# A reworked front for a stencil and mixture-of-experts kernel, with its experts' operands at multiples of 2 KB in SBUF

## The chip, the cores and the metric

One core of a Trainium2 chip runs one program. The metric is device time in microseconds, the median of the runs. Compared are the kernel before and the same kernel with the change below.

## What is computed

The reference takes `x` of shape (8, 128, 128), a step length per batch, and an index per batch. First it makes one explicit step of an advection-diffusion equation on every 128 x 128 grid, and cuts it off at zero:

```
Af = A_grid[None] * f[:, None];  Bf = B_grid[None] * f[:, None]
gradv_Af  = _grad(Af[:, 0], 1) + _grad(Af[:, 1], 2)
gradvv_Bf = _grad2(Bf[:, 0], 1) + _grad2(Bf[:, 1], 2) + _grad(_grad(Bf[:, 2], 2), 1) + _grad(_grad(Bf[:, 2], 1), 2)
x = maximum(f + (-gradv_Af + gradvv_Bf * 0.5) * dt[:, None, None], 0.0)
```

Then each grid is read as 128 tokens of 128 features. `h` is `x` normalised over the features, normalised again over the tokens, and scaled and shifted by `gamma` and `beta`, which a small four-layer network makes from the batch's index. A router picks two of eight experts for each token, and each expert has a hidden layer of 512:

```
gates, idx = top_k(softmax(h @ router_w), 2);  gates = gates / gates.sum(-1)
hid = relu(einsum('nd,edf->nef', h, exp_w1) + exp_b1)
eout = einsum('nef,efd->ned', hid, exp_w2) + exp_b2
out = x + einsum('ned,ne->nd', eout, combine)
```

## The kernel before

Everything is one tile of 128 partitions. The 8 batches are two halves of 4; the 1,024 tokens lie along the free axis. Each engine runs a list of instructions in the order written in its block (`block.sync` for the loads, `block.gpsimd`, `block.scalar`, `block.tensor`, `block.vector`), and semaphores join the lists; nothing is reordered by a planner.

**The front.** Differences along rows and columns are matmuls with two constant matrices, `diff` and `neg_half_diff2`. Each half needs five products of `f` or its transpose `ft` with a grid (`s_b2`, `u_a0`, `u_b0`, `u_a1`, `u_b1`): VectorE makes them for half 0, GpSimd three of them for half 1. `step_cross` makes the inner difference of the mixed term, `cross_operand` its operand `wT`, and `rows_a`, `rows_b`, `columns_b`, `columns_w` add the step up in PSUM (`yt` for half 0, `aux` for half 1). `advance` (L788) multiplies that by the step length and takes `f` away, `relu_step` (L411) cuts it off into `xs`. `feature_stats`, `inverse_sd_features` and `normalise` make `xn`, `norm_transposed` (L586) transposes it, and `token_stats`, `inverse_sd_tokens`, `scale_and_shift` and `conditioned` make `h`. `refined` (L803) is one Newton step for the reciprocal root that ScalarE found by logarithm and exponential. Four small matmuls (`net_layer`, L530) and one pair at L708 and L709 make the style; ScalarE's steps between them are `embedded`, `hyper_first`, `hyper_second`, `style_first` and `softplus`. `step_transposed` and `transposed_step` put the transposed step into `acc`, for the final sum. `keep_warm` (L525) issues matmuls whose result nobody reads.

**The experts.** Expert 0 works in plain fp32, by halves: `layer1_0` (L614) and `layer2_0` (L619), with the second half's front between the first half's matmuls. Experts 1 to 7 work in fp32r with split operands: `h_hi` + `h_lo`, `ws` (weights, high and low part, two slots) and `hid_hi` + `hid_lo`, three matmuls for each product (L625 to L627, and L649, L650, L653). ScalarE makes `hid_hi` and `hid`, VectorE `hid_lo`; hidden layers run three chunks ahead of the output layers. The last expert's output layer is cut into parts of 512, 256 and 256 tokens, `y_last` (L200), so that the stores can start early.

**SBUF.** `sb` (L82) declares a buffer; each takes its bytes in a partition, rounded up to 32, and lies right behind the one declared before it. The operands in question are `h`, `h_hi`, `h_lo` (L133 to L135), and `ws`, `hid`, `hid_hi`, `hid_lo` (L170 to L173).

## Time and profile before

| | us |
|---|---|
| median of 3 runs | 119.5 |
| lowest and highest | 119.18, 119.82 |
| span of the profiled execution | 117.9 |

In the page's part on busy shares an engine's entry is its busy time, the share of the span, and the number of instructions. The line on PEclk cuts the span into 40 equal slices and gives TensorE's granted clock in tenths of full speed; a 9 is 90% or more. In the chain of waits a row is a start, a length and the work that ended last there, in order of time. In a timeline a row is a start, a length and an instruction, or several merged (`x4`); what stands in brackets is the engine's idle time before it and who ended it. An fp32 matmul stands as two records.

### The profile page before, as it was taken

Reading aid. Unit: us, or ns where it says so; the run is one execution under the profiler, and the core shown is the slowest. Engines: PE = TensorE matmul, PEld = TensorE weight load, DVE = VectorE, ACT = ScalarE, POOL = GpSimd, SP = SyncE. Lnnn points to the kernel's source line nnn. Section 1 sums busy time; section 2 is a strip of 40 time slices with the busy share of each in tenths; the row PEclk is TensorE's granted clock in tenths of the full one; section 3 lists DMA queues with packets and bytes.
Section 4 is the critical chain, followed back from the end, with each engine's and each line's share of the span. In section 5 each row is a group of like instructions: output and inputs, shape, how many; then the busy total and the mean of one; then the engine's idle time right before and its main releaser. Section 6 shows DMA issues by size and latency. Waiting matters only on the chain.

```text
span 117.9 us, 1519 instructions
## 1 busy us (share of the span) xinstructions
PE 111.9 (95%) x506; PEld 85.0 (72%) x506; DVE 91.8 (78%) x198; ACT 75.5 (64%) x99; POOL 8.8 (7%) x18
## 2 busy tenths in 40 slices
PE   6999999998999999999999999999999999999960
PEld 2469894446646688888888888888888888888850
DVE  0398789748993496999959976996799589879781
ACT  0403456756361997777777777777777777777800
POOL 1437430000000000000000000000000000000040
PEclk9999999999999999999999999999999999999998
DMA  2999991000000270050400040021004000500004
GB/s 94 310 366 418 407 407 47 0 0 0 0 0 6 96 266 0 8 178 0 178 0 0 29 152 0 0 120 64 0 0 178 0 0 8 170 0 6 0 0 178
DMA packets 4583, 10.86 MB, mean 92 GB/s; under 512 B 800, under 2 KB 1888, under 8 KB 4576
## 3 DMA queue, kind: packets, MB, share of 16 engines
q1 hardware_dynamic: 3920, 9.93, 22.4%
q10 hardware_dynamic: 656, 0.84, 2.3%
q8 instruction: 4, 0.07, 0.2%
q14 instruction: 3, 0.02, 0.1%
HBM read 10.21 MB, written 0.56 MB: 91 GB/s over the span
## 4 chain that ended last, share of the span: by engine, by line
PE 84%; DVE 7%; DMA 4%; issue 1%; ACT 1%; SPq 0%; DVEq 0%
PE zt L625 11%; PE zt L626 11%; PE zt L627 11%; PE zt L614 6%; PE aux L653 6%; PE aux L650 6%; PE aux L649 6%; PE yt L653 5%; PE yt L650 5%; PE yt L649 5%; PE yt L619 4%; DMA gn<-in_grids_dram 4%; DVE st L824 2%; DVE h L853 1%; PE aux L574 1%; PE zt L543 1%
## 5 line engine op out<-in xcount | busy, mean ns | idle before, releaser
L498 ACT ACTIVATE hid_hi<-zt,pv 128x1024 fp32r<-128x1024 f32 x27 | 30.2, 1120 | 17.4 <-PE zt L627 17.3
L945 DVE TENSOR_TENSOR hid_lo<-hid,hid_hi 128x1024 fp32r<-128x1024 f32 x27 | 33.0, 1221 | 10.0 <-issue 5.4
L503 ACT ACTIVATE hid<-zt,pv 128x1024 f32<-128x1024 f32 x27 | 29.9, 1108 | 0.0
L625 PE MATMUL zt<-h_hi,ws 128*128 128x512 f32 x56 | 22.7, 406 | 0.0
L626 PE MATMUL zt<-h_hi,ws 128*128 128x512 f32 x56 | 21.8, 390 | 0.0
L627 PE MATMUL zt<-h_lo,ws 128*128 128x512 f32 x56 | 21.8, 389 | 0.0
L625 PEld LDWEIGHTS zt<-h_hi,ws 128*128 128x128 f32 x56 | 10.5, 188 | 3.0 <-issue 0.5
L626 PEld LDWEIGHTS zt<-h_hi,ws 128*128 128x128 f32 x56 | 10.5, 188 | 2.5 <-issue 0.5
L627 PEld LDWEIGHTS zt<-h_lo,ws 128*128 128x128 f32 x56 | 10.5, 188 | 2.2
L650 PE MATMUL aux<-hid_hi,ws 128*128 128x512 f32 (+1 forms) x32 | 12.0, 376 | 0.0
L649 PE MATMUL aux<-hid_hi,ws 128*128 128x512 f32 (+1 forms) x32 | 12.0, 376 | 0.0
L653 PE MATMUL aux<-hid_lo,ws 128*128 128x512 f32 (+1 forms) x32 | 12.0, 376 | 0.0
L649 PE MATMUL yt<-hid_hi,ws 128*128 128x512 f32 (+1 forms) x28 | 10.5, 374 | 0.0
L650 PE MATMUL yt<-hid_hi,ws 128*128 128x512 f32 (+1 forms) x28 | 10.5, 374 | 0.0
L653 PE MATMUL yt<-hid_lo,ws 128*128 128x512 f32 (+1 forms) x28 | 10.5, 374 | 0.0
L968 DVE TENSOR_TENSOR acc<-acc,yg 128x512 f32<-128x512 f32 x14 | 9.0, 685 | 0.0
L875 DVE TENSOR_TENSOR ws<-we,ws 128x1024 fp32r<-128x1024 f32 x7 | 8.6, 1225 | 0.2
L370 POOL TENSOR_TENSOR acc<-acc,yg 128x512 f32<-128x512 f32 x1 | 1.3, 1272 | 96.3 <-DVE yg L1003 96.3
L614 PE MATMUL zt<-h,we 128*128 128x512 f32 x16 | 7.6, 607 | 0.6 <-DVE h L853 0.6
L619 PE MATMUL yt<-hid,we 128*128 128x512 f32 x16 | 7.5, 592 | 0.0
L528 PE MATMUL zt<-warm 128*128 128x512 bf16 x18 | 6.0, 485 | 1.2 <-DVE warm L775 1.2
L873 DVE CAST ws<-we 128x1024 fp32r<-128x1024 f32 x7 | 4.8, 691 | 2.8 <-PE yt L653 1.4
(136 smaller groups left out, 143.0 us busy)
## 6 DMA issues: line engine op xcount, KB each, us to landing
we<-in_exp_w_dram SPq DMA_DIRECT2D x8, 512.0 KB, 9.1
gate_all<-gates_dram SPq DMA_DIRECT2D x8, 512.0 KB, 3.5
f<-in_x_dram SPq DMA_DIRECT2D x2, 256.0 KB, 4.5
ft<-in_x_exchanged_dram ACTq DMA_DIRECT2D x2, 256.0 KB, 5.3
out_dram<-acc SPq DMA_DIRECT2D x1, 256.0 KB, 2.1
out_dram<-acc SPq DMA_DIRECT2D x2, 128.0 KB, 2.0
first<-d_difference_dt_ids_dram ACTq DMA_DIRECT2D x1, 136.0 KB, 3.2
gn<-in_grids_dram SPq DMA_DIRECT2D x1, 128.0 KB, 4.4
```

The source lines that it names most:

```text
L498: act.activation(hid_hi[:, c, :], zt[c % 2][:], ACT.Relu, bias=bias).then_inc(hi_ready, 1)
L503: act.activation(hid[:, c, :], zt[c % 2][:], ACT.Relu, bias=bias).then_inc(hid_ready, 1)
L614: pe.matmul(z0[c], we[:, 0, 0, c, :], h[:, half(n)], start=True, stop=True).then_inc(z0_ready, 1)
L619: pe.matmul(yt[:, half(n)], we[:, 0, 1, c, :], hid[:, c, half(n)], start=(c == 0), stop=(c == C - 1)).then_inc(l2_0_done, 1)
L625: pe.matmul(zt[c % 2][:, tok], w_hi, h_hi[:, tok], start=True, stop=False)
L626: pe.matmul(zt[c % 2][:, tok], w_lo, h_hi[:, tok], start=False, stop=False)
L627: return pe.matmul(zt[c % 2][:, tok], w_hi, h_lo[:, tok], start=False, stop=True)
L649: pe.matmul(out_ps, w_hi, hid_hi[:, c, tok], start=(c == 0), stop=False)
L650: pe.matmul(out_ps, w_lo, hid_hi[:, c, tok], start=False, stop=False)
L653: return pe.matmul(out_ps, w_hi, hid_lo[:, c, tok], start=False, stop=(c == C - 1))
L945: v.tensor_tensor(hid_lo[:, c, :], hid[:, c, :], hid_hi[:, c, :].bitcast(F32), ALU.subtract).then_inc(lo_ready, 1)
L968: v.tensor_tensor(acc[:, half(n)], acc[:, half(n)], yg[:, half(n)], ALU.add).then_inc(acc_half, 1)
```

## The change

Of the front:

- The loads are dealt out anew between the queues of SP and ACT. `ln_g` and `ln_b` come with the first load, and GpSimd makes four values from them.
- The second half's step is made whole in PSUM. ScalarE scales `diff` and `neg_half_diff2` by minus each batch's step length, an identity matmul puts in `f`, and ScalarE takes the ReLU from PSUM. `advance` remains for half 0 only.
- The Newton steps are folded: the last factor is applied to products made beside the earlier steps. `gamma` is one VectorE operation, no longer four on GpSimd.
- TensorE's order: the transposes of half 0's `xn` come before the style network's last layer and most of half 1's step; those of half 1's `xn` after one `layer2_0`, not two. The first hidden matmul is cut into two pairs of batches. Both `keep_warm` calls behind the first are gone.
- ScalarE's order: see the diff. `cross_product` makes `s_b2` of half 0 in two parts.

Of the layout: two unused buffers, `ahead_of_h` (800 bytes in a partition) and `ahead_of_ws` (1,632 bytes).

The diff, cut to its core:

```diff
-        neg_xp = sb("neg_xp", [P, B, P])
+        diff_dt = sb("diff_dt", [P, BH, P])
+        neg_half_diff2_dt = sb("neg_half_diff2_dt", [P, BH, P])
+        neg_dt = sb("neg_dt", [P, B])
+        neg_xp = sb("neg_xp", [P, BH, P])
...
+        ahead_of_h = sb("ahead_of_h", [P, 200])
         h = sb("h", [P, T])
         h_hi = sb("h_hi", [P, T], F32R)
         h_lo = sb("h_lo", [P, T], F32R)
...
+        ahead_of_ws = sb("ahead_of_ws", [P, 408])
         ws = sb("ws", [P, SLOTS, 2, 2, C, P], F32R)
         hid = sb("hid", [P, C, T])
         hid_hi = sb("hid_hi", [P, C, T], F32R)
...
             load(f[:, 0:BH, :], x[:, 0:BH, :], f_in[0])
             load(gn[:], grids, gn_in)
-            load(gt[:], gridsT, gt_in)
-            load(neg_half_diff2, second_diff, diff2_in)
+            load(ft[:, 0:BH, :], xT[:, 0:BH, :], ft_in[0])
             load(f[:, BH:B, :], x[:, BH:B, :], f_in[1])
+            load(ft[:, BH:B, :], xT[:, BH:B, :], ft_in[1])
+            load(pw[:], p64, p64_in)
+            load(ident, identity, ident_in)
             load(pv[:], p128, p128_in)
...
+            pool.tensor_scalar(gsq[:], ln_g, ln_g, 0.25, ALU.mult, ALU.mult).then_inc(gain_ready, 1)
+            pool.tensor_scalar(quarter_g[:], ln_g, 0.25, None, ALU.mult).then_inc(gain_ready, 1)
+            pool.tensor_scalar(minus_quarter_g[:], ln_g, -0.25, None, ALU.mult).then_inc(gain_ready, 1)
+            pool.tensor_scalar(half_b[:], ln_b, 0.5, None, ALU.mult).then_inc(gain_ready, 1)
...
-            product(u_b0, f, gn[:, 1, :]).then_inc(b0_ready[1], 1)
             pool.wait_ge(ft_in[1], 16)
             pool.wait_ge(gt_in, 16)
             product(u_a1, ft, gt[:, 1, :]).then_inc(a1_ready[1], 1)
+            product(u_b0, f, gn[:, 1, :]).then_inc(b0_ready[1], 1)
+            pool.wait_ge(a0_ready[1], 1)
             product(u_b1, ft, gt[:, 0, :]).then_inc(b1_ready[1], 1)
 
-            pool.wait_ge(glog_ready, 1)
-            step(pool.tensor_tensor(gsum[:], gpos[:], glog[:], ALU.add))
-            step(pool.tensor_scalar(gamma[:], gsum[:], 1e-8, None, ALU.add))
-            pool.wait_ge(p128_in, 16)
-            pool.tensor_scalar(half_gamma[:], gamma[:], 0.5, None, ALU.mult).then_inc(gamma_ready, 1)
-            pool.tensor_scalar(gamma_g[:], gamma[:], ln_g, 0.25, ALU.mult, ALU.mult).then_inc(gamma_ready, 1)
...
-            act.dma_start(ft[:, 0:BH, :], xT[:, 0:BH, :]).then_inc(ft_in[0], 16)
-            act.dma_start(pw[:], p64).then_inc(p64_in, 16)
-            act.dma_start(ft[:, BH:B, :], xT[:, BH:B, :]).then_inc(ft_in[1], 16)
-            act.dma_start(ident, identity).then_inc(ident_in, 16)
+            act.dma_start(gt[:], gridsT).then_inc(gt_in, 16)
+            act.dma_start(neg_half_diff2, second_diff).then_inc(diff2_in, 16)
             act.preload_act_table_set("natural_log_exp_and_others")
+
+            def scaled_differences():
+
+                act.wait_ge(first_in, 16)
+                act.activation(neg_dt[:], dtb, ACT.Copy, scale=-1.0).then_inc(neg_dt_ready, 1)
+                act.wait_ge(neg_dt_ready, 1)
+                for b in range(BH, B):
+                    act.activation(diff_dt[:, b - BH, :], diff, ACT.Copy, scale=neg_dt[:, b:b + 1]).then_inc(diff_dt_ready, 1)
+                act.wait_ge(diff2_in, 16)
+                for b in range(BH, B):
+                    act.activation(neg_half_diff2_dt[:, b - BH, :], neg_half_diff2, ACT.Copy,
+                                   scale=neg_dt[:, b:b + 1]).then_inc(diff2_dt_ready, 1)
...
+            def relu_whole_step(k):
+
+                act.wait_ge(df_ready, BH // 2 + k + 1)
+                b = BH + 2 * k
+                act.activation(xs[:, b:b + 2, :].rearrange("p b j -> p (b j)"), pair_of(1, k),
+                               ACT.Relu).then_inc(xs_ready, 1)
...
             act.wait_ge(const_ready, 2)
+            scaled_differences()
+            relu_step(0)
             embedded()
-            relu_step(0)
             relu_step(2)
             hyper_first()
+            inverse_sd_features(0)
             hyper_second()
-            inverse_sd_features(0)
+            normalise(0)
             style_first()
-            normalise(0)
             softplus()
             inverse_sd_tokens(0)
             transposed_step(0)
             conditioned(0)
-            relu_step(4)
-            relu_step(6)
+            relu_whole_step(0)
+            relu_whole_step(1)
             hidden0(0, 0)
...
             inverse_sd_tokens(1)
+            conditioned(1)
             transposed_step(1)
-            conditioned(1)
...
+            def whole_step_input(k):
+
+                pe.wait_ge(ident_in, 16)
+                pe.wait_ge(f_in[1], 16)
...
+                pe.matmul(pair_of(1, k), ident, f[:, b:b + 2, :].rearrange("p b j -> p (b j)"),
+                          start=True, stop=False, skip_group_check=True)
+
+            def whole_step_rows_b():
+
+                pe.wait_ge(b0_ready[1], 1)
+                pe.wait_ge(diff2_dt_ready, BH)
+                for b in range(BH, B):
+                    pe.matmul(own(b), neg_half_diff2_dt[:, b - BH, :], u_b0[:, b, :], start=False, stop=False,
+                              skip_group_check=True)
...
+                pe.wait_ge(a0_ready[1], 1)
+                for b in range(BH, B):
+                    pe.matmul(own(b), diff_dt[:, b - BH, :], u_a0[:, b, :], start=False, stop=False,
+                              skip_group_check=True)
...
+            def whole_step_columns_w():
+
+                pe.wait_ge(w_op_ready, 2)
+                pe.wait_ge(diff_dt_ready, BH)
+                for b in range(BH, B):
+                    pe.matmul(own(b), wT[:, b, :], diff_dt[:, b - BH, :], start=False, stop=False, skip_group_check=True)
...
+            def whole_step_columns_b(k):
+
+                pe.wait_ge(b1_ready[1], 1)
+                for b in of_pair(1, k):
+                    last = pe.matmul(own(b), u_b1[:, b, :], neg_half_diff2_dt[:, b - BH, :], start=False, stop=True,
+                                     skip_group_check=True)
+                last.then_inc(df_ready, 1)
...
+            def layer1_0_by_pairs():
+
+                for k, made in enumerate((h_ready, h_act_ready)):
+                    pe.wait_ge(made, 2)
+                    tok = slice(2 * k * P, 2 * (k + 1) * P)
+                    last = pe.matmul(z0[0][:, tok], we[:, 0, 0, 0, :], h[:, tok], start=True, stop=True)
+                last.then_inc(z0_ready, 1)
...
-            rows_b(1, 0, start=True)
+            whole_step_input(0)
             pe.wait_ge(p128_in, 16)
             net_layer(2, pv[:, HW2_AT:HW2_AT + SH], hyp1[:], SH)
-            rows_b(1, 1, start=True)
+            whole_step_input(1)
             net_layer(3, pv[:, SW1_AT:SW1_AT + SE], hyp2[:], SE)
-            columns_w(1, 0, final=False)
+            whole_step_rows_b()
+            pe.wait_ge(xp_ready, BH)
+            norm_transposed(0)
             pe.wait_ge(net_sb, 4)
             pe.matmul(small[:, 0:B], pw[:, SW2_AT:SW2_AT + P], sty1[:], start=True, stop=True)
             pe.matmul(small[:, B:2 * B], pw[:, SW2_AT + P:SW2_AT + 2 * P], sty1[:], start=True,
                       stop=True).then_inc(net_ps, 1)
-            columns_w(1, 1, final=False)
-            pe.wait_ge(ident_in, 16)
-            pe.wait_ge(xp_ready, BH)
-            norm_transposed(0)
-            columns_b(1)
+            whole_step_columns_w()
+            whole_step_rows_a()
             step_transposed(0)
-            rows_a(1, start=False)
-
-            keep_warm(WARM_H[0])
-            wait_for_h(0)
+            whole_step_columns_b(0)
+            whole_step_columns_b(1)
+
             pe.wait_ge(net_sb, 6)
+            pe.wait_ge(w_in[0], 16)
+            layer1_0_by_pairs()
             pe.wait_ge(acc_ready, 1)
-            pe.wait_ge(w_in[0], 16)
-            for c in range(C):
+            for c in range(1, C):
                 layer1_0(0, c)
             layer2_0(0, 0)
-            layer2_0(0, 1)
-            pe.wait_ge(xp_ready, B)
+            pe.wait_ge(xs_ready, BH)
             norm_transposed(1)
-            layer2_0(0, 2)
-            layer2_0(0, 3)
+            for c in range(1, C):
+                layer2_0(0, c)
             step_transposed(1)
             logits(0)
-            keep_warm(WARM_H[1])
             wait_for_h(1)
...
-            def refined(n, variance, eps, rough, sq, vs, rs):
+            def normalise(n):
 
                 hb = batches(n)
-                then(v.tensor_tensor(sq[:, hb], rough[:, hb], rough[:, hb], ALU.mult))
-                then(v.scalar_tensor_tensor(vs[:, hb], variance, eps, sq[:, hb], ALU.add, ALU.mult))
-                then(v.scalar_tensor_tensor(rs[:, hb], vs[:, hb], 3.0, rough[:, hb], ALU.subtract, ALU.mult))
-
-            def normalise(n):
-
                 v.wait_ge(var1_ready, BH * (n + 1))
                 v.wait_ge(rs1_ready, n + 1)
-                refined(n, mv1[:, batches(n), 1], 1e-5, rough1, sq1, vs1, rs1)
-                v.scalar_tensor_tensor(mrs1[:, batches(n)], mv1[:, batches(n), 0], -1.0, rs1[:, batches(n)], ALU.mult,
+                squared = mark(v.tensor_tensor(sq1[:, hb], rough1[:, hb], rough1[:, hb], ALU.mult))
+                mark(v.scalar_tensor_tensor(rm1[:, hb], mv1[:, hb, 0], -1.0, rough1[:, hb], ALU.mult, ALU.mult))
+                v.wait_ge(dve, squared)
+                then(v.scalar_tensor_tensor(vs1[:, hb], mv1[:, hb, 1], 1e-5, sq1[:, hb], ALU.add, ALU.mult))
+                v.scalar_tensor_tensor(rs1[:, hb], vs1[:, hb], 3.0, rough1[:, hb], ALU.subtract,
+                                       ALU.mult).then_inc(rs1_final, 1)
+                v.scalar_tensor_tensor(mrs1[:, hb], vs1[:, hb], 3.0, rm1[:, hb], ALU.subtract,
                                        ALU.mult).then_inc(mrs1_ready, 1)
+                v.wait_ge(rs1_final, n + 1)
                 for b in range(n * BH, n * BH + XN_DVE):
                     v.tensor_scalar(xn[:, b, :], xs[:, b, :], mv1[:, b, 0:1], rs1[:, b:b + 1], ALU.subtract,
...
                 v.tensor_scalar(ve2[:, batches(n)], mv2[:, batches(n), 1], gsq[:, 0:1], 1e-8, ALU.mult,
                                 ALU.add).then_inc(var2_ready, 1)
-                then(v.tensor_scalar(mh[:, batches(n)], mv2[:, batches(n), 0], minus_half_g[:, 0:1], ln_b, ALU.mult,
-                                     ALU.add))
-                v.wait_ge(gamma_ready, 2)
-                return mark(v.scalar_tensor_tensor(tg[:, batches(n)], mh[:, batches(n)], ln_b, half_gamma[:, batches(n)],
-                                                   ALU.subtract, ALU.mult))
+                last = mark(v.tensor_scalar(mh[:, batches(n)], mv2[:, batches(n), 0], minus_quarter_g[:, 0:1],
+                                            half_b[:, 0:1], ALU.mult, ALU.add))
+                if n == 0:
+                    v.wait_ge(glog_ready, 1)
+                    v.wait_ge(net_sb, 5)
+                    last = mark(v.scalar_tensor_tensor(gamma[:], gpos[:], 1e-8, glog[:], ALU.add, ALU.add))
+                v.wait_ge(dve, last)
+                return mark(v.scalar_tensor_tensor(tg[:, batches(n)], mh[:, batches(n)], half_b[:, 0:1],
+                                                   gamma[:, batches(n)], ALU.subtract, ALU.mult))
...
-                refined(n, ve2[:, hb], 0.0, rough2, sq2, vs2, rs2)
+                squared = mark(v.tensor_tensor(sq2[:, hb], rough2[:, hb], rough2[:, hb], ALU.mult))
+                mark(v.scalar_tensor_tensor(rg2[:, hb], rough2[:, hb], quarter_g[:, 0:1], gamma[:, hb], ALU.mult,
+                                            ALU.mult))
                 v.wait_ge(dve, moved)
-                shifted = mark(v.tensor_tensor(shift0[:, hb], tg[:, hb], rs2[:, hb], ALU.mult))
-                v.tensor_tensor(scale[:, hb], rs2[:, hb], gamma_g[:, hb], ALU.mult).then_inc(shift_ready, 1)
+                mark(v.tensor_tensor(rt2[:, hb], rough2[:, hb], tg[:, hb], ALU.mult))
+                v.wait_ge(dve, squared)
+                then(v.tensor_tensor(vs2[:, hb], ve2[:, hb], sq2[:, hb], ALU.mult))
+                shifted = mark(v.scalar_tensor_tensor(shift0[:, hb], vs2[:, hb], 3.0, rt2[:, hb], ALU.subtract, ALU.mult))
+                v.scalar_tensor_tensor(scale[:, hb], vs2[:, hb], 3.0, rg2[:, hb], ALU.subtract,
+                                       ALU.mult).then_inc(shift_ready, 1)
                 v.wait_ge(dve, shifted)
                 v.wait_ge(net_sb, 6)
                 v.tensor_tensor(shift[:, hb], shift0[:, hb], beta[:, hb], ALU.add).then_inc(shift_ready, 1)
...
+            cross_product(0)
+            cross_product(1)
...
-            advance(0)
-            v.wait_ge(p128_in, 16)
-            mark(v.tensor_scalar(gsq[:], ln_g, ln_g, 0.25, ALU.mult, ALU.mult))
-            squared = mark(v.tensor_scalar(minus_half_g[:], ln_g, -0.5, None, ALU.mult))
+            advance()
...
             product(u_a0, f, 1, gn[:, 0, :]).then_inc(a0_ready[1], 1)
-            v.wait_ge(dve, squared)
             moved = token_stats(0)
             scale_and_shift(0, moved)
             conditioned(0)
-            advance(1)
             feature_stats(1)
```

## Rows read from the trace of the kernel before

**Rows 1.** The page: busy time of the engines, and granted clock by slice.
```profile
PE 111.9 (95%) x506; PEld 85.0 (72%) x506; DVE 91.8 (78%) x198; ACT 75.5 (64%) x99; POOL 8.8 (7%) x18
...
PEclk9999999999999999999999999999999999999998
```

**Rows 2.** TensorE in two stretches: length, busy, instructions, clock, DMA share, GB/s.
```profile
29.18:113.90 84.72, 84.69 (x372) 1.00 0.14 51
5.50:19.60 14.10, 13.67 (x89) 1.00 0.91 351
```

**Rows 3.** The chain of waits, in the front.
```profile
1.16 4.36 DMA gn<-in_grids_dram
...
8.54 0.89 PE yt L568 x8
...
18.66 0.74 DVE h L853 x2
19.57 3.67 PE zt L614 x8
...
29.18 1.10 PE zt L614 x2
```

**Rows 4.** Timeline of TensorE in the front.
```profile
7.41 1.13 PE L561 MATMUL yt<-u_b,neg_half_diff 128*128 128x256 f32 x4
...
13.15 0.28 PE L533 MATMUL zt<-hyp,pv 128*64 128x8 f32 x2
...
15.09 0.60 PE L594 MATMUL yt<-ident,xn 128*128 128x128 f32 x4
...
17.72 1.67 PE L528 MATMUL zt<-warm 128*128 128x512 bf16 x7
...
24.80 0.60 PE L594 MATMUL aux<-ident,xn 128*128 128x128 f32 x4
...
28.20 0.59 PE L528 MATMUL zt<-warm 128*128 128x512 bf16 x2
```

**Rows 5.** The DMA view: KB, and us from issue to landing.
```profile
gn<-in_grids_dram SPq DMA_DIRECT2D x1, 128.0 KB, 4.4
```

**Rows 6.** Timeline of VectorE in the front.
```profile
10.96 0.20 DVE L915 TENSOR_SCALAR gsq<-pv 128x1 f32<-128x1 f32 x1
...
11.14 0.87 DVE L798 BATCH_NORM_STATS2 st<-xs 128x6 f32<-128x128 f32 x4
12.05 0.38 DVE L801 BATCH_NORM_AGGREGATE mv<-st 128x2 f32<-128x6 f32 x4
...
17.68 0.16 DVE L806 TENSOR_TENSOR sq<-rough 128x4 f32<-128x4 f32 x1
...
19.31 1.12 DVE L792 SCALAR_TENSOR_TENSOR neg_xp<-aux,first,f 128x128 f32<-128x128 f32 x4
```

**Rows 7.** Timeline of ScalarE in the front.
```profile
12.89 0.28 ACT L419 ACTIVATE lv<-mv,eps_ln 128x4 f32<-128x4 f32 x1
...
17.55 0.58 ACT L447 ACTIVATE acc<-zt 128x512 f32<-128x512 f32 x1
```

**Rows 8.** Timeline of TensorE in the block and in the last expert.
```profile
42.80 0.39 PE L625 MATMUL zt<-h_hi,ws 128*128 128x512 f32 x1
...
44.16 0.39 PE L649 MATMUL aux<-hid_hi,ws 128*128 128x512 f32 x1
...
110.89 0.40 PE L649 MATMUL aux<-hid_hi,ws 128*128 128x512 f32 x1
111.13 0.40 PE L650 MATMUL aux<-hid_hi,ws 128*128 128x512 f32 x1
...
112.64 0.28 PE L649 MATMUL aux<-hid_hi,ws 128*128 128x256 f32 x1
...
113.00 0.28 PE L649 MATMUL yt<-hid_hi,ws 128*128 128x256 f32 x1
...
113.36 0.28 PE L649 MATMUL yt<-hid_hi,ws 128*128 128x256 f32 x1
```

## What the change was predicted to do

> **What bounds the kernel now.** I read the page's busy shares first: TensorE (PE) is busy for 95% of the span, at a granted clock of nine tenths or more in nearly every slice [rows 1]. The chain of waits then says from when. It follows one load and a string of short links through VectorE (DVE), ScalarE (ACT) and PE until 29.18 us, where the second half's `h` reaches PE [rows 3]; behind that point PE is busy for 84.69 of 84.72 us, to the last matmul [rows 2]. So the kernel is a front of 29.18 us, a closed block of PE work of 84.7 us, and an end of 4.0 us (117.9 - 113.9). The time falls by what the start of the block moves forward, and by what changes inside the block. The profiled execution spans 117.9 us, the median run is 119.5 us; I keep the 1.6 us between them.
>
> **The block.** Nothing in it is reordered. What changes is where its operands lie. In the kernel before, a buffer starts at the next multiple of 32 bytes behind the one declared before it; this puts `h`, `h_hi` and `h_lo` 1,056 bytes past a multiple of 2,048, and `ws`, `hid`, `hid_hi` and `hid_lo` 1,568 bytes past one. With the declarations that are added and dropped and the two pads of 800 and 1,632 bytes, all of them come to 0. So every 512-column operand (2,048 bytes) crosses a 2,048-byte line before, and none does after. Six block matmuls stand between the starts 42.80 and 44.16, which is 226.7 ns each [rows 8]. The last expert tests whether the crossing is what costs: it has operands of 256 columns, those of the `aux` part run from 1,568 across the line to 2,592, those of the `yt` part from 544 to 1,568, inside it. Three `aux` ones take from 112.64 to 113.00, and three `yt` ones from there to 113.36 [rows 8]: 0.12 us each, on either side. The distances between moving operand and weights don't change modulo 512 bytes either. I cost the edit at 0 for 324 matmuls of 512 columns and 24 of 256. Its bounds are not closed by this: only an absolute start of 32 modulo 64 bytes has been seen for these operands, and none of 0. Below, a bf16 matmul of the same 512 columns comes every 0.216 us (seven in 1.67, two in 0.59) [rows 4], 10.7 ns less, which makes 348 x 10.7 = -3.7 us; above, two block matmuls once stand 0.24 apart (110.89 to 111.13) [rows 8], and 348 x 8 to 13 ns would be +2.9 to +4.6 us. I take 0, since the row that varies the crossing shows no effect.
>
> The Trainium skill ("TensorE: Matmul & The Clock Gate", section "Back-to-back issue gap") gives N/2.4 + 2.5 ns for a matmul at full clock, 215.8 ns for 512 columns. By it the block's 226.7 ns is not the engine's own pace, and something, of which the start address is one candidate, would be giving 10.9 ns back; the bf16 rows agree with the page, the block's rows do not.
>
> **The front, first half, up to the transposes of `xn`.** (a) The loads are dealt out anew. `gn` lands 4.4 us after its issue, at 5.5 us [rows 3, 5], with the 256 KB of `ft` behind `first` on ACT's queue; now only the 128 KB of `gt` ride there, and `neg_half_diff2` is issued third on ACT instead of fourth on SP. `rows_b` had started at 7.41, when it had landed [rows 4]. `gn` may gain nothing or 0.4 us, the stall behind `neg_half_diff2` another 0.15; I take -0.5, bounds -0.1 and -0.7. The eight scaled matrices are 8 ACT operations of about 0.4 us plus one small one, 3.5 us on an ACT queue that holds nothing else until 10.6; if `neg_half_diff2` were late they end by 9, still in that cover. (b) `gsq` and `minus_half_g` leave DVE for GpSimd (POOL): 11.14 - 10.96 = -0.18 [rows 6]; POOL has 2.5 us to spare there. (c) `inverse_sd_features(0)` stood behind `hyper_second`: its first operation ran at 12.89 [rows 7], the variances were there at 12.43 (12.05 + 0.38) [rows 6]. Now it is ahead: -0.45. Together -1.1 on the DVE and ACT side. PE had to give as well, since the transposes at 15.09 came straight behind `columns_w(1, 1)` [rows 4]: between network layer 3 (13.15) [rows 4] and 15.09 it did two groups of 4 matmul records, four small ones and their bubbles, now one group of 8, which costs 0.89 [rows 3] and 0.1 to refill. I take -1.15 for the transposes, at 13.95.
>
> **First half, from there to the hidden layer.** (d) `refined` was three dependent steps of 0.2 us and two more (17.68 to 18.66) [rows 3, 6]; its last step is folded into `scale` and `shift0`: -0.15. POOL's four operations for gamma go, for one DVE step of 0.2 us beside `mh`; in turn the style network's last layer is behind the transposes, so the logarithm ends some 0.1 before it is used. Nothing on balance, at worst +0.3. (e) A new cost: `step_transposed(0)` is now behind `whole_step_columns_w` and `whole_step_rows_a`, 0.89 us each. ACT's copy of its result, 0.58 us, ran in the gap at 17.55 while DVE made the scales [rows 7]. Now it gets its input at about 17.1 and stands in ACT's queue ahead of the two `h` of `conditioned(0)`, which are due at 17.2: +0.35, bounds 0 and +0.6. DVE's two `h` aren't behind it, and `layer1_0_by_pairs` lets PE begin with them, but PE's next 0.43 us need ACT's pair. So the second pair starts at 19.57 - 1.15 - 0.15 + 0.35 = 18.62. `keep_warm(7)` only filled the wait (17.72 to 19.4) [rows 4]: removed at no gain.
>
> **Second half.** (f) The step is now whole inside PSUM, so DVE's four `neg_xp`, 1.12 us [rows 6], go and the two ReLUs follow ACT's `h` directly: the features side comes 1.4 us earlier and has `xn` by 22.75 (24.15 before). (g) The transposes of `xn` move ahead of one more `layer2_0` (0.86 us): they start at 18.62 + 0.43 + 2.58 + 0.86 + 0.1 = 22.6, held to 22.75, against 24.80. From them to `layer1_0(1, 0)` it took 29.18 - 24.80 = 4.38; less 0.15 as in (d), `h` is ready at 27.0. (h) But PE itself: from the start of these transposes to the second `keep_warm` it went from 24.80 to 28.20 [rows 4], 3.4 us of dense work; now one `layer2_0` of 0.86 more lies there: 22.75 + 3.4 + 0.86 = 27.0, and 0.1 for a bubble. The two meet; what is late next is PE itself, and the second `keep_warm` (0.43, at 28.20) has no room to be missed. The block starts at 27.1 instead of 29.18: **-2.1 us**. With (a) and (e) at their bounds it is -0.9 to -2.8. Inside the block `h_hi`, `h_lo` and the first split weights follow `h` at the old distance, and their matmuls wait for them 2 us less than they have to spare.
>
> The sum: 117.9 - 2.1 + 0 = 115.8 us of span, and with 1.6 us around it 117.4 us. By its own bounds, 116.7 to 118.6.
>
> **The rivals.** *The block speeds up*: if the start address is what holds the matmuls at 226.7 ns, they fall to 216: 117.4 - 3.7 = 113.7 us. For it speaks the bf16 row; against it the last expert's two kinds of start. *The block slows down*, the one that ends on the other side: with all operands at the same 2,048-byte phase, the moving read, the weight load behind it and the writes of DVE and ACT may meet in the same place. It decides from 2.1 us / 348 = 6 ns a matmul on; at 0.235 us each, which PE shows only when it starts anew [rows 8], it is +2.9: 120.3 us. Against it: `hid`, its parts and `ws` shared one phase before as well. *The front gains little*: the ACT queue takes the place of DVE. The copy of (e) and `hidden0(0, 0)` (0.67 us) stand ahead of the two small operations on which the second half's `xn` hangs, and `gn` may land no earlier; then the block starts at 28.3 to 29.2, and the time is 118.6 to 119.5 us. *The clock falls*: PE now has nine warming matmuls less and waits of 0.3 us between small network layers. The clock stayed full over the 14.1 us of this stretch with 13.67 busy [rows 2]; with PE at the lower of its two levels for the first group of the hidden layer, its 3.67 us [rows 3] double, some +2.9 us after what the other engines hide: 120.3 us. The Trainium skill (same page, section "HAM oscillation — how this bites in real kernels") warns of gaps between bursts, which speaks against taking these matmuls out; no row here shows a fall.
>
> **How the numbers follow.** The forecast of 117.4 has 0.62, a front that gains little 0.18, a faster block 0.10, a slower block 0.06, the clock 0.04. The range 116.2 to 119.5 leaves out the last three, 0.20 together. A measurement of this kernel can tell about 0.5% (0.6 us) from no change: faster is 0.62 + 0.10 + a third of 0.18 = 0.78, same 0.12, slower 0.10.
>
> **What would show it.** In the profile after: the last DVE-waiting `layer1_0` start at 27.1; the `h` rows of DVE near 17.2 and 26; no `neg_xp` of the second half; the copy of `zt` to `acc` just before ACT's first `h`; six block matmuls in 1.36 us. If they take 1.30 or 1.41, the block's part is wrong; if the start is beyond 28.3, so is the front's, most likely at (e) or (a).

## The result, and the profile after

The changed kernel took 117.48 us (117.08 to 118.07, 4 runs) beside 119.34 us for the kernel before (119.16 to 119.82, 4 runs): a ratio of 0.984, with a 95% interval of 0.980 to 0.987. The forecast was 117.4. The profiled execution took 117.48 us and spans 115.7 us; before it was 117.9 us. The ratios here and below leave out executions more than 1.5% longer than the fastest of their kernel, two in all: one of 120.78 us with the late transposes and one of 121.65 us with the new loads.

The page of the kernel after, its first part and the granted clock, beside [rows 1]:

```profile
PE 110.6 (96%) x511; PEld 85.7 (74%) x511; DVE 90.5 (78%) x198; ACT 78.0 (67%) x108; POOL 9.5 (8%) x18
...
PEclk9999999999999999999999999999999999999997
```

The chain of waits of the kernel after, in part, from its beginning to the start of the block, beside [rows 3] (start, length, what ended last):

```profile
1.17 3.93 PE zt L559 x9
...
5.13 1.13 PE zt L574 x8
...
17.50 0.89 PE aux L640 x8
...
26.46 0.79 PE yt L671 x8
27.26 0.97 PE zt L679 x2
```

The chain of before ran over a load, VectorE and ScalarE; this one is TensorE alone from 5.13 us on. No other engine stands in it any more. Small waits remain inside its groups, which the chain doesn't name (0.23 us at the first `h`, below). The timeline of TensorE in the front has the milestones that the prediction named, beside [rows 4] (start, length, instruction):

```profile
5.13 1.13 PE L574 MATMUL zt<-first,s_b 128*128 128x128 f32 x8
6.10 1.03 PE L582 MATMUL yt<-u_a,first 128*128 128x256 f32 x4
...
13.87 0.67 PE L660 MATMUL yt<-ident,xn 128*128 128x128 f32 x4
...
18.24 1.34 PE L686 MATMUL zt<-h,we 128*128 128x256 f32 x4
...
22.85 0.60 PE L660 MATMUL aux<-ident,xn 128*128 128x128 f32 x4
...
27.12 1.10 PE L679 MATMUL zt<-h,we 128*128 128x512 f32 x2
```

So the block starts at 27.12 us instead of 29.18 [rows 2], 2.06 us sooner, and the rest of the span is as long as it was: the second half's first `layer1_0` to the last matmul, in the view by stretches (stretch, length, busy, clock, DMA share, GB/s), beside the first row of [rows 2]:

```profile
27.12:111.81 84.69, 84.67 (x374) 1.00 0.14 51
```

### The profile page after: what moved, and what is told of

Read it like the earlier page. It is cut to its first block, busy times and chain, and to the rows that moved or that the text cites. A ratio compares the mean times of both kernels' runs of the same rounds, so it can differ in the third digit from the quotient of the medians.

```text
span 115.7 us, 1540 instructions
## 1 busy us (share of the span) xinstructions
PE 110.6 (96%) x511; PEld 85.7 (74%) x511; DVE 90.5 (78%) x198; ACT 78.0 (67%) x108; POOL 9.5 (8%) x18
## 3 DMA queue, kind: packets, MB, share of 16 engines
HBM read 10.21 MB, written 0.56 MB: 93 GB/s over the span
## 4 chain that ended last, share of the span: by engine, by line
PE 96%; DVE 1%; DVEq 0%; issue 0%
PE zt L698 11%; PE zt L699 11%; PE zt L700 11%; PE yt L692 6%; PE aux L723 6%; PE aux L722 6%; PE aux L726 6%; PE zt L679 5%; PE yt L723 5%; PE yt L722 5%; PE yt L726 5%; PE zt L559 3%; PE zt L574 2%; PE yt L671 1%; PE zt L686 1%; PE aux L619 1%
## 5 line engine op out<-in xcount | busy, mean ns | idle before, releaser
L722 PEld LDWEIGHTS aux<-hid_hi,ws 128*128 128x128 f32 x32 | 6.0, 188 | 1.2
L723 PEld LDWEIGHTS aux<-hid_hi,ws 128*128 128x128 f32 x32 | 6.0, 188 | 1.2
```

What stands on the lines that cost most here:

```text
L722: pe.matmul(out_ps, w_hi, hid_hi[:, c, tok], start=(c == 0), stop=False)
L723: pe.matmul(out_ps, w_lo, hid_hi[:, c, tok], start=False, stop=False)
```

## The experiments

Two questions. Does the layout edit do anything, since the block neither gained nor lost? And do the steps of the front work as they were costed? All runs keep the whole computation. In the table below a buffer's place is its start in a partition modulo 2,048 bytes, and a block stretch always holds the same 288 matmuls, from the start of the 23rd split-weight matmul to that of the 311th: 287 of 512 columns and one of 256. The kernel before took 119.6 to 119.7 us in the sessions of these runs, beside 119.34 when the changed kernel was measured. So kernels of different sessions are compared by their ratios.

### The layout

**The changed front without the pads.**

```
-        ahead_of_h = sb("ahead_of_h", [P, 200])
-        ahead_of_ws = sb("ahead_of_ws", [P, 408])
```

> The changed kernel without its two pads: h and its parts start 1,248 bytes, ws and the hid buffers 1,664 bytes past a multiple of 2,048. Theory (the start address costs nothing): six block matmuls in 1.36 us as before and after, block start near 27.1 us, median 117.5 us. Rival (the pads repair a slower block that the new declarations made): six take 1.40 us or more, and the time is 119 us or more.

119.81 us, ratio 1.002 (0.999 to 1.004). The whole gain is gone, though the block starts at 27.44 us. Its matmuls come more slowly, so the rival held.

**The changed front with the operands where they stood before** (`h` and its parts at 1,056, `ws` and `hid` at 1,568): the pads are `[P, 464]` and `[P, 24]`.

> The changed kernel with pads that put h at 1,056 and ws and the hid buffers at 1,568 bytes past a multiple of 2,048, as in the kernel before: the front's edits alone. Theory: 117.5 us, six block matmuls in 1.36 us. Rival (a part of the gain is the layout's): between 118 and 119.3 us.

118.01 us, ratio 0.985 (0.981 to 0.990): the gain is there without any multiple of 2 KB. The time lies at the edge of the rival's range, but the layout isn't what puts it there: the block stretch is the same (below). In the profiled execution the block starts 0.51 us later than in the kernel after, and TensorE's first group alone takes 0.53 us more (6.62 - 5.12 = 1.50 us, against 0.97).

**The kernel before with its operands at multiples of 2 KB**, by pads of 248 and 384 elements at the same two places.

> The kernel before with two pads (992 and 1,536 bytes) that put all the experts' operands at multiples of 2,048 bytes: the layout's edit alone. Theory: 119.4 us, no change, 1.36 us for six. Rival: 118.8 us or less.

119.68 us, ratio 0.999 (0.997 to 1.002). For the kernel before, this layout is worth nothing.

**One distance only: `ws` at 288**, everything else at 0.

```
-        ahead_of_ws = sb("ahead_of_ws", [P, 408])
+        ahead_of_ws = sb("ahead_of_ws", [P, 480])
+        ahead_of_hid = sb("ahead_of_hid", [P, 440])
```

> The changed kernel with ws 288 bytes past a multiple of 2,048 and everything else at one, so that weights and moving operands no longer stand at the same place modulo 512 bytes, and the weights are at 32 modulo 64. Theory (neither absolute nor relative places matter): 117.5 us, 1.36 us for six. Rival (the relative place matters, and was the same in both kernels): another spacing, 1.30 us (113.8 us in all) if 226.7 ns was already the slow one, 1.40 us or more (119 us or more) if it was the fast one.

119.75 us, ratio 1.001 (0.998 to 1.004): the relative place matters, and 226.7 ns was the faster pace.

**All at 1,664**, the place that `ws` and `hid` had without pads: `ahead_of_h` is `[P, 104]`, and `ahead_of_ws` stays at 408.

> The changed kernel with h, h_hi, h_lo, ws, hid, hid_hi and hid_lo all 1664 bytes past a multiple of 2,048 (1664 is where ws and hid stood in the kernel without pads, e1_after_no_pads; there h stood at 1248). Theory A, what counts is that the weights and the moving operand of a block matmul stand at one and the same place modulo 512 bytes, wherever that is: every spacing in the block falls back to 226.7 ns (544 periods of 2.4 GHz) and the time to 117.5 us (117.2 to 118.1), ratio 0.984 to 0.990. Theory B, what counts is where ws itself stands (fast at 0 and 32 modulo 512, as in the runs so far, slow at 128 and 288): the spacing stays at 231 to 233 ns, as in the hid groups of e1_after_no_pads, where ws and hid stood equal and the mean was 231.4 ns, and the time at 119.2 to 119.9 us, ratio about 1.000. Theory C, that only multiples of 2 KB are sure: as B. I hold A at 55 in 100.

117.56 us, ratio 0.984 (0.978 to 0.989), as by theory A.

**`ws` at 64**, everything else at 0: pads `[P, 200]`, `[P, 424]`, and `ahead_of_hid` with 496 elements.

> The changed kernel with ws alone moved to 64 bytes past a multiple of 2,048; h, h_hi, h_lo, hid, hid_hi and hid_lo at 0. The fast kernels so far had weights and moving operands at equal places modulo 512 bytes, and the slow ones had them 288 (e4_after_ws_288) and 96 (the h groups of e1_after_no_pads) bytes apart: both are 32 more than a multiple of 64. Theory A1, the two need only agree modulo 64 bytes: spacing 226.7 ns and 117.5 us (117.2 to 118.1), ratio 0.984 to 0.990. Theory A2, they must agree more coarsely than that (modulo 128, 256 or 512): spacing 233.3 ns (560 periods of 2.4 GHz) and 119.7 us (119.2 to 119.9), ratio 0.997 to 1.004. I hold A1 at 50 in 100.

120.18 us, ratio 1.003 (1.001 to 1.005), as by theory A2.

The same 288 block matmuls in these kernels, one row of the view by stretches each. In this order: the kernel after, the old places, all at 1,664 (the fast ones); without pads, `ws` at 288, `ws` at 64 (the slow ones):

```profile
40.26:105.43 65.17, 65.17 (x289) 1.00 0.16 58
```

```profile
40.80:105.97 65.17, 65.17 (x289) 1.00 0.16 57
```

```profile
40.22:105.38 65.16, 65.16 (x289) 1.00 0.17 59
```

```profile
40.62:107.54 66.92, 66.92 (x289) 1.00 0.16 58
```

```profile
40.55:107.63 67.08, 67.08 (x289) 1.00 0.15 57
```

```profile
40.81:107.90 67.09, 67.09 (x290) 1.00 0.15 56
```

TensorE is busy throughout at a clock of 1.00 in all six, and still 1.75 to 1.92 us go. The profile names no wait for it; each matmul comes a little later behind the last. Six of them in the kernel with `ws` at 64, and six in the kernel after:

```profile
44.08 0.40 PE L699 MATMUL zt<-h_hi,ws 128*128 128x512 f32 x1
...
45.48 0.40 PE L723 MATMUL aux<-hid_hi,ws 128*128 128x512 f32 x1
```

```profile
43.44 0.39 PE L698 MATMUL zt<-h_hi,ws 128*128 128x512 f32 x1
...
44.80 0.39 PE L722 MATMUL aux<-hid_hi,ws 128*128 128x512 f32 x1
```

45.48 - 44.08 = 1.40 us against 1.36: 233.3 ns each instead of 226.7. In one table (the mean is over the 287 gaps of 512-column matmuls in the stretch; the times are of several sessions):

| kernel | `h` parts | `ws` | `hid` parts | distance, modulo 512 | ns a matmul | median, us |
|---|---|---|---|---|---|---|
| before | 1056 | 1568 | 1568 | 0 | 226.7 | 119.34 |
| before, at 2 KB | 0 | 0 | 0 | 0 | 226.7 | 119.68 |
| after | 0 | 0 | 0 | 0 | 226.7 | 117.48 |
| after, old places | 1056 | 1568 | 1568 | 0 | 226.7 | 118.01 |
| after, all at 1,664 | 1664 | 1664 | 1664 | 0 | 226.7 | 117.56 |
| after, no pads | 1248 | 1664 | 1664 | 96 for `h` | 232.8 | 119.81 |
| after, `ws` at 288 | 0 | 288 | 0 | 288 for all | 233.3 | 119.75 |
| after, `ws` at 64 | 0 | 64 | 0 | 64 for all | 233.3 | 120.18 |

What decides is not where an operand stands but where weights and moving operand stand towards each other. The absolute place is out: 0, 1,056/1,568 and 1,664 are all fast. Crossing a line of 2,048 bytes is out too, since all 512-column operands of the kernel at 1,664 cross one. A distance of 64, 96 or 288 bytes is slow, a multiple of 512 is fast. Since all weight tiles of a slot lie 512 bytes apart and serve the same moving operand, no coarser step than 512 can matter; whether 128 or 256 would do wasn't tried.

The price falls on the matmuls of 512 columns alone. The last expert's last twelve have 256; their first and last start, in the kernel after and in the one with `ws` at 288:

```profile
110.20 0.28 PE L722 MATMUL aux<-hid_hi,ws 128*128 128x256 f32 x1
...
111.51 0.28 PE L726 MATMUL yt<-hid_lo,ws 128*128 128x256 f32 x1
```

```profile
112.43 0.28 PE L723 MATMUL aux<-hid_hi,ws 128*128 128x256 f32 x1
...
113.74 0.28 PE L727 MATMUL yt<-hid_lo,ws 128*128 128x256 f32 x1
```

Both are 1.31 us for eleven steps, 119 ns each; with `ws` at 64 it is 1.29 us (112.66 to 113.95).

Two things stay open. The first is the mechanism: the runs show the distance that costs, but not whether TensorE's two reads meet or something else does. The second: without pads `hid` and `ws` stand at the same place, yet their matmuls are slow too (a mean of 231.4 ns, those with `h` 234.2). With `h` moved to that place as well, all are at 226.7. Either a group of `h` matmuls slows the group of `hid` matmuls behind it, or the distance between `h` and `hid` counts as well; in the other two slow kernels these two stand at the same place. These runs don't separate the two.

### The front

**Both `keep_warm` calls put back** (`keep_warm(7)` ahead of `layer1_0_by_pairs`, `keep_warm(2)` behind `logits(0)`).

> The changed kernel with both groups of warming matmuls put back, seven ahead of the first hidden matmul and two behind the logits of half 0. Theory (TensorE itself is the last to be ready in the changed front, so nothing hides them): 7 x 0.216 less about 0.15 of wait, and 2 x 0.216, is +1.8 us: block start 28.9 us, 119.3 us. Rival (there is slack of other engines' making left, as in the kernel before): at most +0.6 us.

119.33 us, ratio 0.996 (0.993 to 0.999): 0.012 of 119.7 us, 1.5 us of the gain, are lost, near the 1.8 that the theory gave. The same nine matmuls taken out of the kernel before:

> The kernel before without its nine warming matmuls behind the first stage. Theory (they only fill waits): 119.4 us, block start 29.2 us, granted clock full. Rival (they keep the clock up): the lower of the two clock levels shows in the slices behind them, six block matmuls or the first hidden ones take up to twice as long, 120.3 us or more.

119.66 us, ratio 1.001 (0.998 to 1.002). So they cost nothing before and 1.5 of their 1.9 us (9 x 0.216) after. The chain of the kernel after with `keep_warm` back shows why; they are on it:

```profile
18.27 1.46 PE zt L559 x6
19.73 0.86 PE zt L686 x4
...
28.27 0.45 PE zt L559 x2
28.71 0.43 PE zt L679
```

And without them the clock doesn't fall in the kernel before. It ran at this granted clock, and the first hidden group behind a wait of 1.68 us takes 3.51 us to the next group's start (22.76 - 19.25), as with them (23.08 - 19.57):

```profile
core 0: 117.5 us, clock 1.000
```

```profile
19.25 3.67 PE L614 MATMUL zt<-h,we 128*128 128x512 f32 x8 [1.68 <-ACT h L441]
```

**The transposes of half 1's `xn` behind two `layer2_0`**, as before the change.

```
             layer2_0(0, 0)
+            layer2_0(0, 1)
             pe.wait_ge(xs_ready, BH)
             norm_transposed(1)
-            for c in range(1, C):
+            for c in range(2, C):
```

> The changed kernel with the transposes of half 1's xn after two layer2_0 again, not one. Theory (h of half 1 and TensorE meet within 0.1 us at the block's start): h comes 0.86 us later, and TensorE waits for it: +0.8 us, block start 27.9 us, 118.3 us. Rival (TensorE's amount of work alone sets the start): 0, 117.5 us.

118.28 us, ratio 0.987 (0.982 to 0.992). TensorE now reaches the block first and waits for `h`:

```profile
24.46 0.60 PE L660 MATMUL aux<-ident,xn 128*128 128x128 f32 x4
...
28.73 0.67 PE L679 MATMUL zt<-h,we 128*128 128x512 f32 x1 [0.72 <-DVE h L938]
```

From the transposes to the block it is 4.27 us, as in the kernel after (27.12 - 22.85). So in the kernel after TensorE's list and the making of `h` end together, and one more `layer2_0` ahead of the transposes goes through whole.

This profiled execution is the one of 120.78 us; the other three took 118.06 to 118.34. It lost a further 1.7 us behind the block's start, where six matmuls of `layer1_0` take 4.35 us (30.48 to 34.83) instead of 2.66 (28.87 to 31.53 in the kernel after). The granted clock was low there (stretch, length, busy, clock, DMA share, GB/s):

```profile
30.48:34.83 4.35, 4.35 (x8) 0.61 0.00 0
```

The front readings lie ahead of that stretch and aren't touched by it. Whether the wait of 0.72 us brought the fall on isn't shown: waits of 0.83 us at the same place and of 1.68 us, in the kernel before without its fillers, were followed by none.

**ScalarE's copy of the step behind its two `h`** (`conditioned(0)` ahead of `transposed_step(0)`).

> The changed kernel with ScalarE's copy to acc behind its two h of half 0, not ahead of them. Theory: the h pair is ready at 18.1 us, not 18.8, TensorE's bubbles of 0.3 us there shrink to 0.1: -0.2 us, 117.3 us. Rival (the copy is awaited by the second hidden matmul, or the ReLUs behind it are late next): 0 or up to +0.4 us.

117.99 us, ratio 0.986 (0.981 to 0.991). The 117.3 of the theory didn't come; what the edit did is read from the profile below.

**`hyper_second` and `style_first` of ScalarE back ahead of the features' work.**

```
-            inverse_sd_features(0)
             hyper_second()
-            normalise(0)
+            inverse_sd_features(0)
             style_first()
+            normalise(0)
```

> The changed kernel with ScalarE's old order of half 0: inverse_sd_features(0) behind hyper_second, normalise(0) behind style_first. Theory: the logarithm runs at 12.4 to 12.5 us, not 11.9; the transposes of xn and all behind them come 0.5 us later: 118.0 us. Rival (TensorE's rows_b group, which ends just before the transposes, covers it): 0 to +0.1 us.

118.21 us, ratio 0.986 (0.980 to 0.992).

None of these three ratios is clear of the changed kernel's own 0.984 (0.980 to 0.987), so what follows rests on one profiled execution of each. Nor can they be read from the start of the block alone, because the profiled executions differ in something else: TensorE's first group of eight took 0.97 us in the kernel after (5.13 to 6.10, above), and 1.84 us with the copy late, 1.64 us with ScalarE's order back, 1.68 us with the late transposes. The copy's kernel, timeline of TensorE:

```profile
5.00 2.05 PE L574 MATMUL zt<-first,s_b 128*128 128x128 f32 x8
6.84 1.09 PE L582 MATMUL yt<-u_a,first 128*128 128x256 f32 x4
...
14.66 0.67 PE L660 MATMUL yt<-ident,xn 128*128 128x128 f32 x4
...
19.03 1.10 PE L686 MATMUL zt<-h,we 128*128 128x256 f32 x4
19.97 2.74 PE L679 MATMUL zt<-h,we 128*128 128x512 f32 x6
...
23.40 0.60 PE L660 MATMUL aux<-ident,xn 128*128 128x128 f32 x4
```

The eight records stand 0.21 us apart here and 0.11 us in the kernel after, half the pace until 6.8 us. That is the ratio of the engine's two clock levels, and I take it for the lower one, though the row of the granted clock reads 1.00 here. It is the same code up to there. With TensorE last from 5 us on, this delay goes through to the block whole, as in the kernel with the old places, and it has to be taken off before the edit can be read. So the later intervals decide. The first hidden group takes 0.94 us (19.97 - 19.03) instead of 1.17 (19.41 - 18.24, the kernel after): the copy costs TensorE 0.23 us where it stands ahead of ScalarE's `h`. From the first `xn` transposes to that group's start it is 4.37 us in both. For ScalarE's order, the start of the first group is later by 0.33 us and the group itself longer by 0.67; behind that its milestones are 15.05, 19.64, 24.26 and 28.53:

```profile
15.05 0.90 PE L660 MATMUL yt<-ident,xn 128*128 128x128 f32 x4
...
28.53 0.67 PE L679 MATMUL zt<-h,we 128*128 128x512 f32 x1
```

28.53 - 27.12 - 0.33 - 0.67 = 0.41 us for the order. For the late transposes 28.73 - 27.12, less 0.05 and 0.71, is 0.85 us, one `layer2_0`.

**The new order of the loads in the kernel before.**

```
-            load(gt[:], gridsT, gt_in)
-            load(neg_half_diff2, second_diff, diff2_in)
-            load(f[:, BH:B, :], x[:, BH:B, :], f_in[1])
+            load(ft[:, 0:BH, :], xT[:, 0:BH, :], ft_in[0])
+            load(f[:, BH:B, :], x[:, BH:B, :], f_in[1])
+            load(ft[:, BH:B, :], xT[:, BH:B, :], ft_in[1])
+            load(pw[:], p64, p64_in)
+            load(ident, identity, ident_in)
...
-            act.dma_start(ft[:, 0:BH, :], xT[:, 0:BH, :]).then_inc(ft_in[0], 16)
-            act.dma_start(pw[:], p64).then_inc(p64_in, 16)
-            act.dma_start(ft[:, BH:B, :], xT[:, BH:B, :]).then_inc(ft_in[1], 16)
-            act.dma_start(ident, identity).then_inc(ident_in, 16)
+            act.dma_start(gt[:], gridsT).then_inc(gt_in, 16)
+            act.dma_start(neg_half_diff2, second_diff).then_inc(diff2_in, 16)
```

> The kernel before with the loads dealt out over the two queues in the changed order (ln_g and ln_b still with the 128-row parameters). Theory: gn lands 0.3 to 0.7 us earlier, the stall behind neg_half_diff2 goes, block start 28.7 us, -0.5 us: 118.9 us. Rival (something behind it, TensorE's rows in half 0 or the later products, takes the gain back): -0.1 us or less.

119.63 us, ratio 0.999 (0.995 to 1.002). Its timeline of TensorE, and its DMA view:

```profile
5.47 1.13 PE L543 MATMUL zt<-first,s_b 128*128 128x128 f32 x8 [0.37 <-DVE s_b L780]
...
7.38 1.13 PE L561 MATMUL yt<-u_b,neg_half_diff 128*128 128x256 f32 x4
...
15.06 0.60 PE L594 MATMUL yt<-ident,xn 128*128 128x128 f32 x4
```

```profile
first<-d_difference_dt_ids_dram ACTq DMA_DIRECT2D x1, 136.0 KB, 3.8
gn<-in_grids_dram SPq DMA_DIRECT2D x1, 128.0 KB, 3.6
...
neg_half_diff<-n_second_difference_dram ACTq DMA_DIRECT2D x1, 64.0 KB, 5.7
```

The rival held. `gn` lands 0.8 us sooner than in [rows 5] (3.6 us from its issue; in the kernel before without fillers, with the old loads, it is 3.7 as well, so most of this is no matter of the order). But `first` is later (3.8 us from its issue, 3.2 before), so that `step_cross` starts at 5.47, and `neg_half_diff2` is no sooner, so that `rows_b` starts at 7.38, where it was 7.41 [rows 4]. The transposes of `xn` are at 15.06 (15.09 before). In the kernel after, issued at the same time in the same order, `neg_half_diff2` needed 4.5 us. Why it took 5.7 here stays open.

## Why the prediction was right

**The total and its path: right.** 115.7 us of span against 115.8 forecast, 117.48 us against 117.4. The milestones: transposes of half 0 at 13.87 (13.95 forecast), of half 1 at 22.85 (22.75), the block at 27.12 (27.1). "What is late next is PE itself" holds, and earlier than I had it, from 5.13 us and not only from the second half: put back, the nine fillers move the block from 27.12 to 28.55 us, although TensorE's first matmuls started 0.17 us sooner in that execution. The other kernels with this front say the same. Where the first group takes 0.97 us, the block starts 21.98 or 21.99 us behind `step_cross`: 27.12 - 5.13 in the kernel after, 27.44 - 5.46 without pads, 27.38 - 5.39 with `ws` at 288, 27.07 - 5.09 at 1,664, 27.63 - 5.64 with `ws` at 64. What varies between executions is when `step_cross` starts and at what pace. That the profiled execution met the forecast to 0.1 us is therefore partly luck: with the same front the block starts anywhere from 27.07 to 27.63 us.

**(a) the loads: the size held, what makes it is more than their order.** I took -0.5 us, and -1.15 for the whole way to the transposes of `xn`. Half 0's step ends where the network's first layer begins, in the kernel before and in the one after:

```profile
10.25 0.28 PE L533 MATMUL zt<-onehot,pw 32*64 32x8 f32 x2
```

```profile
9.71 0.28 PE L564 MATMUL zt<-onehot,pw 32*64 32x8 f32 x2
```

That is -0.54 us. `step_cross` starts 0.22 us later (4.91 before, 5.13 after), but the waits for `u_a0` and `neg_half_diff2` are gone: from `step_cross` to this row it took 5.34 us and takes 4.58. From here to the transposes it is 4.16 us instead of 4.84 (15.09 in [rows 4]): another -0.68 from TensorE's own order and from ScalarE's, which has `xn` ready for it (with ScalarE's old order the transposes are 0.18 us later, 15.05 - 13.87 less the two delays). Together -1.22. The order of loads alone, in the kernel before, brought nothing: there `step_cross` was at 5.47 and `rows_b` still waited. Two things differ: in the kernel after, VectorE makes `s_b` for `step_cross` in two parts, and `neg_half_diff2` took 1.2 us less to land. So the loads' share rests on the whole change, and no run shows it alone. Its size isn't sure either: that row starts at 9.95 to 10.25 us in the three profiles with the old loads and front, and at 9.53 to 10.21 in the six with the new ones and a first group of 0.97 us. What holds in all of these six is the missing waits: 4.57 or 4.58 us from `step_cross` to this row, where the old ones take 4.69 to 5.34.

**(b), (c), (d).** `gsq` is made on GpSimd at 7.82 us, far ahead of its use. Undoing ScalarE's order (c, with `style_first`) costs 0.41 us; I had 0.45 on that side. From the transposes to VectorE's `h` it takes 3.49 us (17.36 - 13.87) instead of 3.57 (18.66 - 15.09), half of the 0.15 of (d). The folded Newton step and `gsq` weren't tried alone.

**(e) the copy: right in kind, 0.23 us instead of 0.35, and the step around it 0.26 us off.** It stands where I put it, waits for TensorE, and ends last ahead of ScalarE's pair of `h`:

```profile
17.53 0.60 ACT L477 ACTIVATE acc<-zt 128x512 f32<-128x512 f32 x1 [1.08 <-PE zt L649]
18.03 0.80 ACT L471 ACTIVATE h<-yt,shift,scale 128x128 f32<-128x128 f32 x2
```

TensorE's second pair of batches starts here:

```profile
18.88 0.70 PE L686 MATMUL zt<-h,we 128*128 128x256 f32 x2
```

The forecast had 18.62. I had let ScalarE's `h` alone set this point; VectorE's `h` was being made from 17.36 on, but TensorE's own list ran to 18.24. From the second pair to the transposes of half 1 it takes 3.97 us (22.85 - 18.88) instead of the 4.13 that I added up, and so the milestones behind it agree again to 0.1.

**The fillers: "removed at no gain" holds for the kernel before (1.001) and not for the new order (0.996 instead of 0.984).** I costed the removal against the waits of before; the cover was what the rest of the change took away.

**(f) to (h): right.** The second half's features side is early enough, and with one more `layer2_0` ahead of the transposes `h` comes 0.72 us too late for TensorE. That the clock doesn't fall was right for the four executions of this kernel (117.08 to 118.07 us). The rival is real all the same: with the late transposes one execution in four had the fall, for about 1.7 us.

**The block at 0: right, for one of two reasons.** The sentence that carries is the one I gave second: "the distances between moving operand and weights don't change modulo 512 bytes". The crossing of the 2,048-byte line agrees with the result (0.999 for the kernel before at multiples of 2 KB) but isn't what matters. The last expert's 256-column matmuls, my test for it, couldn't have shown a cost of placement: they come every 119 ns in the slow kernels too. What I missed is the comparison in between. The front's new and dropped declarations move every buffer behind them; without the pads `h` would stand 96 bytes off `ws` modulo 512, the block would lose 1.75 us in the stretch shown, and the kernel would be at 119.81. So the layout edit is worth about 2 us beside the same front without it, and nothing beside the kernel before: 0.018 in the ratios, or 2.1 us. The profiled spans differ by 2.2 us, 1.8 of them in the block and 0.3 by a first load that landed later in that execution. The rival "the block slows down" gave 0.235 us a matmul, near the 0.2328 to 0.2333 of the slow kernels, and had the condition reversed: I had feared that equal places collide, and it is unequal ones that cost. The rival "speeds up to 216 ns" falls: no layout went below 226.7.

The Trainium skill ("SBUF — State Buffer", section "Who interferes with whom") has it that TensorE has two independent read ports, one for the moving operand and one for the weights, and never waits on anyone. It says nothing on placement. Read as a rule that TensorE's reads are never held up, it would leave no layout a cost, and the trace disagrees: 6.7 ns a matmul, 65.17 against 67.09 us over 288.

## What to carry to other kernels

A new or dropped buffer is part of a change even when nobody reads it: it shifts what is declared behind it. Where TensorE streams fp32r matmuls of 512 columns back to back, with a weight load each, hold weights and moving operands a multiple of 512 bytes apart, and compare the spacing of the matmuls in the block whenever the list of buffers changes; the busy share and the clock don't show it. Cost the removal of a filler against the waits that the new order leaves, not those of the old. And before a row is used as a test, ask whether the effect would show in it at all: matmuls of 256 columns don't feel the placement.

## What was not expected of the hardware

- Relative place: 64, 96 or 288 bytes between weights and moving operand, modulo 512, cost 6.1 to 6.7 ns for each matmul of 512 columns (226.7 to 232.8 or 233.3 ns), at a granted clock of 1.00 and with TensorE 100% busy. Those of 256 columns come every 119 ns either way.
- TensorE's rise to full clock at the beginning comes at a different time in each execution. The same nine bf16 matmuls from 1.17 us on stand ahead of `step_cross` in every kernel here; then its eight matmuls come 0.11 us apart or 0.21 us, and the group takes 0.97 to 1.84 us. The nine themselves come 0.43 us apart to 4.13 us, where those in the waits of the kernel before come every 0.216. The PEclk line reads 9 in these slices either way, so only the spacing shows it. In the kernel after, which has no slack behind it, that is up to 0.9 us of the time, beside a gain of 2.06. The Trainium skill ("TensorE: Matmul & The Clock Gate", section "What's actually happening") says that the number of cold matmuls varies between runs of one kernel; the traces agree as far as kernels with the same code up to there can show it.
- With the late transposes, one execution of four had the granted clock at 0.61 over 30.48 to 34.83 us, right behind the block's start, and lost 1.7 us. What brought it on isn't shown.
